# Graph attention and mixture of experts on one core: the second product three tiles behind the first, its results in three banks, ScalarE's output in four slots, rows turned sooner, and GpSimd's sends paced by the first products

## What is computed

```python
# x: 64 graphs x 128 nodes x 128 features; adj: 64 x 128 x 128
x = x + gnn(layernorm(x), adj, W, a)            # one graph attention layer
y = layernorm(x)
probs = softmax(y @ gate_w + gate_b)            # 16 experts
top_probs, top_idx = top_k(probs, 2)            # two experts for each node
gates = top_probs / sum(top_probs)
hidden = silu(y @ w1[e]) * (y @ w2[e])          # e: the expert, 128 -> 256
x = x + sum over both experts of gate * (hidden @ w3[e])
```

## Time and profile before

| | |
|---|---|
| median of three runs | 521.4 us (519.5 to 524.1) |
| the profiled execution | 522.0 us, span 520.2 us |
| PE / DVE / ACT / POOL busy | 395.9 / 250.4 / 226.7 / 257.1 us |
| attention part | to about 165 us |
| first pass of the experts | first product 168.3 us, last send 353.3 us |
| second pass | rows turned from 360.2 us, last send 513.7 us |
| granted clock of TensorE, mean | 0.913 |

### The profile page before, as it was taken

One profiled execution on the slowest core, in us unless ns is written; L12 is line 12 of the kernel. 1 busy time (PEld: TensorE's weight loads), 2 busy tenths in 40 slices (PEclk: granted clock), 3 DMA queues, 4 the chain that ended last, 5 costly groups with the idle time before them and its releaser, 6 DMA issues.

```text
span 520.2 us, 11474 instructions
## 1 busy us (share of the span) xinstructions
PE 395.9 (76%) x2993; PEld 358.6 (69%) x2994; DVE 250.4 (48%) x978; ACT 226.7 (44%) x583; POOL 257.1 (49%) x284
## 2 busy tenths in 40 slices
PE   6789788777786564488888798872988888788782
PEld 3578677665675464488788697762888878778781
DVE  4788989858676323324342343340342433333341
ACT  2789686656465212224342343330443443333430
POOL 5222256765357575334555545551355555455454
PEclk9999999978786776879999999995999899999996
DMA  3544445546462365686675666524654655555410
GB/s 109 150 135 126 119 134 173 162 152 205 116 197 97 112 216 190 218 258 212 216 223 165 200 198 201 173 70 111 207 176 148 190 173 182 163 156 187 151 33 2
DMA packets 75547, 83.35 MB, mean 160 GB/s; under 512 B 10564, under 2 KB 60111, under 8 KB 75504
## 3 DMA queue, kind: packets, MB, share of 16 engines
q1 hardware_dynamic: 66032, 61.58, 39.1%
q0 software_dynamic: 9472, 21.26, 11.6%
HBM read 36.06 MB, written 28.94 MB: 125 GB/s over the span
## 4 chain that ended last, share of the span: by engine, by line
PE 49%; DVE 14%; issue 14%; SPq 6%; ACT 5%; DMA 4%; another core or an unknown queue 3%; ACTq 2%; POOL 1%; POOLq 0%; DVEq 0%
PE bank L494 26%; PE bank L504 11%; PE bank L366 4%; SPq L298 3%; ACT em L626 2%; PE bank L414 2%; PE bank L416 2%; DVE stats L682 2%; DMA shared<-in_adj_dram 2%; DVE R L738 1%; PE bank L423 1%; DVE h L692 1%; DVE prob L929 1%; DVE R L935 1%
## 5 line engine op out<-in xcount | busy, mean ns | idle before, releaser
L494 PE MATMUL bank<-xT,w_t 128*128 128x128 f32 x1280 | 180.5, 287 | 14.7 <-DVE prob L929 7.6
L494 PEld LDWEIGHTS bank<-xT,w_t 128*128 128x128 f32 x1280 | 164.8, 201 | 18.6 <-DVE prob L929 9.7
L929 DVE TENSOR_TENSOR prob<-em,bank 128x256 f32<-128x256 f32 x160 | 67.3, 420 | 181.1 <-ACT em L626 110.9
L626 ACT ACTIVATE em<-bank 128x256 f32<-128x256 f32 x160 | 59.8, 382 | 184.5 <-PE bank L494 127.9
L504 PE MATMUL bank<-W,prob 128*128 x640 | 104.3, 287 | 40.4 <-DVE R L935 38.6
L504 PEld LDWEIGHTS bank<-W,prob 128*128 128x128 f32 x640 | 87.3, 198 | 48.8 <-issue 48.7
L1030 POOL DMA_INDIRECT out_dram<-R x80 | 78.3, 978 | 82.1 <-DVE R L935 62.6
L1030 POOL DMA_INDIRECT sorted_rows<-R x80 | 78.4, 980 | 79.8 <-DVE R L935 60.4
L1008 POOL DMA_INDIRECT sorted_rows<-R,ROW x64 | 62.7, 980 | 26.2 <-issue 17.6
L935 DVE SCALAR_TENSOR_TENSOR R<-bank,R 128x128 f32<-128x128 f32 x160 | 55.4, 346 | 33.4 <-PE bank L504 28.0
L999 POOL TENSOR_TENSOR rstd<-var_eps,half_neg 128x4 f32<-128x4 f32 x32 | 32.4, 1022 | 68.4 <-DVE var_eps L698 65.4
(11 more groups left out here) (129 smaller groups left out, 384.6 us busy)
## 6 DMA issues: line engine op xcount, KB each, us to landing
R<-sorted_rows SPq DMA_DIRECT2D x160, 130.0 KB
w_t<-W SPq DMA_DIRECT2D x80, 256.0 KB
W<-in_L_ffn_w_dram SPq DMA_DIRECT2D x48, 128.0 KB
sorted_rows<-pad SPq DMA_DIRECT2D x34, 130.0 KB
R<-in_x_dram SPq DMA_DIRECT2D x16, 256.0 KB
shared<-in_adj_dram SPq DMA_DIRECT2D x16, 256.0 KB
sorted_rows<-R POOLq DMA_INDIRECT x80
out_dram<-R POOLq DMA_INDIRECT x80
```

The costliest lines, as they stand in the source:

```text
L494: ins = nc.tensor.matmul(H[k][:, m * P:(m + 1) * P], w_t[:, par, k, m * P:(m + 1) * P], xT[:, par, k * P:(k + 1) * P], start=True, stop=True)
L626: nc.scalar.activation(sil[:, k % 2, :], H[k][:, 0:HC * P], ACT.Silu).then_inc(silu_ready, 1)
L929: V.tensor_tensor(hidT[:, k, :], sil[:, k % 2, :], H[k][:, HC * P:2 * HC * P], ALU.mult).then_inc(hid_ready, 1)
```

## The change

- `LAG, NO = 3, 3`: the second product and the adding stand three tiles behind the first instead of two, and the results rotate through banks 5, 6 and 7. `down` waits for `row_ready` of tile t - 3.
- `sil` has four slots (in `hT`) instead of two; `silu` waits for `hid_ready` of t - 4 instead of t - 2.
- `turn_rows` and `copy_rows` move from k = 1 to k = 0.
- Since bank 7 is now a result bank, tables 1 and 2 are turned into the bank that the first second product of quads 1 and 2 is about to use, and read from it just ahead of that tile's add.
- Five of the 25 last dispatches wait for first products: tiles 47, 51, 55, 59 and 63 for 1, 2, 5, 8 and 11 of them.

```diff
+    LAG, NO = 3, 3
-        sil = em[:].rearrange("p (k m) -> p k m", m=HC * P)
+        sil = hT[:].rearrange("p a (k m) -> p (a k) m", m=HC * P)
+        def out_bank(c, at, k):
+            return (at % RB * QT + k + c * NT) % NO
-            XP, H, O = bank[0], bank[1:5], bank[5:7]
+            XP, H, O = bank[0], bank[1:5], bank[5:5 + NO]
-            def down(c, q, k, e):
+            def down(c, q, at, k, e):
                 t = q * QT + (c * NT + k)
+                o = O[out_bank(c, at, k)]
                 pe.wait_ge(hid_ready, t + 1)
-                if c or later(q, 1) or k >= 2:
-                    pe.wait_ge(row_ready, t - 1)
+                if c or later(q, 1) or k >= NO:
+                    pe.wait_ge(row_ready, t - (NO - 1))
+                if c == 0 and isinstance(q, int) and q in (1, 2) and k == 0:
+                    turn_table(q, o)
...
-                        if k == 1 and not last:
+                        if k == 0 and not last:
                             turn_rows(c, q + 1, (at + 1) % RB, nth + (at + 1) // RB)
-                        if k >= 2:
-                            down(c, q, k - 2, e[k - 2])
+                        if k >= LAG:
+                            down(c, q, at, k - LAG, e[k - LAG])
                         elif not first:
-                            down(c, q - 1, k + 2, e_last[k])
+                            down(c, q - 1, at + RB - 1, k + (QT - LAG), e_last[k])
...
             def silu(t, k):
                 act.wait_ge(up_done, t + 1)
-                if later(t, 2):
-                    act.wait_ge(hid_ready, t - 1)
+                if later(t, QT):
+                    act.wait_ge(hid_ready, t - (QT - 1))
...
-                        if k == 1 and not last:
+                        if k == 0 and not last:
                             copy_rows(c, q + 1, 1 - par)
...
-                        if k >= 2:
-                            add_row(c, t + (k - 2), at % RB, k - 2)
+                        if k >= LAG:
+                            add_row(c, t + (k - LAG), at, k - LAG,
+                                    table=q if c == 0 and isinstance(q, int) and q in (1, 2) and k == LAG else None)
...
+            PACED = {8: 1, 12: 2, 16: 5, 20: 8, 24: 11}
             for m in range(t, NG):
+                if m - t in PACED:
+                    pool.wait_ge(up_done, PACED[m - t])
                 dispatch(m)
```

More of the change, by code:

```diff
@@ L623, in silu @@
                 act.wait_ge(up_done, t + 1)
[L624 to L626 removed]
+                if later(t, QT):
+                    act.wait_ge(hid_ready, t - (QT - 1))
+                nc.scalar.activation(sil[:, k, :], H[k][:, 0:HC * P], ACT.Silu).then_inc(silu_ready, 1)
             def copy_up(k, par, e):
@@ L857, in read_table @@
                 dve.wait_ge(cols_turned, l + 1)
-                V.tensor_copy(EID[0:1, first:first + ahead], RT[0:1, TABLE_AT[l][0]:TABLE_AT[l][0] + ahead])
-                V.tensor_copy(BLK[0:1, first:first + n], RT[0:1, TABLE_AT[l][1]:TABLE_AT[l][1] + n]).then_inc(table_ready, 1)
+                V.tensor_copy(EID[0:1, first:first + ahead], source[0:1, TABLE_AT[l][0]:TABLE_AT[l][0] + ahead])
+                V.tensor_copy(BLK[0:1, first:first + n], source[0:1, TABLE_AT[l][1]:TABLE_AT[l][1] + n]).then_inc(table_ready, 1)
             full, ceil = t_f[:, 0, :], t_f[:, 1:3, :].rearrange("p c e -> p (c e)")
@@ L903, in aside @@
                     columns(2, tile_no)
-                if q == 1 and k == 3:
-                    read_table(1)
-                if q == 3 and k == 0:
-                    read_table(2)
             first_stats(0, 0)
@@ L921, in _ @@
             count_rows()
-            H, O = bank[1:5], bank[5:7]
+            H, O = bank[1:5], bank[5:5 + NO]
             def gate_hidden(t, k):
@@ L928, in gate_hidden, with add_row @@
                     dve.wait_ge(down_done, t - (QT - 1))
-                V.tensor_tensor(hidT[:, k, :], sil[:, k % 2, :], H[k][:, HC * P:2 * HC * P], ALU.mult).then_inc(hid_ready, 1)
-            def add_row(c, t, slot, k):
+                V.tensor_tensor(hidT[:, k, :], sil[:, k, :], H[k][:, HC * P:2 * HC * P], ALU.mult).then_inc(hid_ready, 1)
+            def add_row(c, t, at, k, table=None):
                 dve.wait_ge(down_done, t + 1)
-                r = rows[:, slot * QT + k, :]
-                V.scalar_tensor_tensor(r[:, D:2 * D], O[k % 2][:, 0:D], r[:, GATE + c:GATE + c + 1], r[:, D:2 * D],
+                o = O[out_bank(c, at, k)]
+                if table is not None:
+                    read_table(table, o)
+                r = rows[:, at % RB * QT + k, :]
+                V.scalar_tensor_tensor(r[:, D:2 * D], o[:, 0:D], r[:, GATE + c:GATE + c + 1], r[:, D:2 * D],
                                        ALU.mult, ALU.add).then_inc(row_ready, 1)
@@ L949, in quad @@
                     if last:
-                        for k in (2, 3):
-                            add_row(c, t + k, at % RB, k)
+                        for k in range(QT - LAG, QT):
+                            add_row(c, t + k, at, k)
                 list_run(dve, quad, peel=(c == 0))
```

19 lines of the change are left out of this document (8 added, 11 removed).

## The result

The changed kernel takes 514.49 us, the median of six runs (509.41 to 519.98), the kernel before on the same chip 520.09 (six runs, 516.93 to 524.1). The ratio is 0.988, with a 95% interval of 0.984 to 0.993. Timed once more on another chip the ratio was 0.984 (0.979 to 0.989). So the change is faster by 1.2 to 1.6 %, where 3.3 % was forecast. The ratios leave out executions that fell into a slower state of the chip, so they are not always the quotient of the two medians beside them.

A forecast was written before the change was run, and what follows sets the result against it. The prediction took PE's signals, held back during bursts of GpSimd sends, to bound the kernel. From 522.0 us, -11 (steady), -9 (dispatches) and +2.6 (tails) gave 504.6, stated as 504.5; own range 490 to 515, with rivals 484 to 525.

The forecast's parts named there:

- What bounds the kernel: Both passes: bursts of GpSimd sends hold back PE's signals, so some 0.4 us of each tile are waiting, 140 tiles long.
- The steady term: Both passes, 140 tiles: a lag of three saves 0.08 us a tile, -11 us; bounds 0 and -56.
- cycles of five: Signals, burst, next signals: five sends for four, 8.93 us for five tiles where four took 7.65; one cycle in four keeps four.
- The transposes' place: Turning rows and their copy one place sooner in each quad takes back some saving: 0.04 us a tile.
- The paced dispatches: First pass's start: pauses in GpSimd's dispatches free SP's padding writes, so quad 4 loads sooner: -9 us, bounds -2 and -13.
- With both halves at 12.80 us, SP is through 8.0 us sooner: SP's 32 padding blocks before quad 4's load: the first 16 fall from 20.81 us to the others' 12.80.
- Tails: End of each pass: one send more behind the last product, 2 x 1.28 = +2.6 us.
- PE without waits: Rival: delayed signals come just in time and sends are single; 474 us, or 486 with six tiles a cycle; 15 in 100.
- Burst unchanged: Rival: the cycle keeps four tiles; 515.6 us, or 524.6 without the dispatches' gain; 15 in 100.
- The slower restart: Rival: copy and register load delay each cycle's restart; 9.9 us for five tiles, 525 to 535 us; 10 in 100.
- The first rival: PE runs nearly without waits: up to 1.55 us a tile for 474 us, 1.70 for 486; 15 in 100.
- The sum: Whole execution: 522.0 - 11 - 9 + 2.6 = 504.6 us, stated as 504.5.

The follow-up runs named there:

- few sends: Kernel before, with the sends of three tiles of four left out in the second pass: 494.56 us in one run against 528.74.
- thin sends: Kernel before, second pass's sends moving 16 bytes of each row instead of 512, to a scratch tensor: 525.48 us in one run against 528.74.
- The two pairs: Rows turned behind the quad's second tile again, on the changed kernel (0.977 for 0.984) and with padding dealt out and pauses kept (0.967 for 0.973).
- dealt-out padding: Changed kernel, SP's 16 second-pass padding writes moved from ahead of quad 4's load to two behind each of eight later loads: 0.973; without pauses 0.970.

## Why the prediction was right and wrong

**What bounds the kernel: right.** PE's signals wait for an end of GpSimd's sends. With few sends the lateness was gone (0.08 us) and PE ran at 1.45 us a tile; with thin sends it stayed. The third bank without the lag gave nothing (0.997). The Trainium skill's Perfetto Trace Analysis (Optimization Strategy) says that consistent bubbles can mean too little PSUM for the next tile; for PE's stops at second products this is not the cause here. Whether more banks would help the first products, ahead of which most stops stand with the lag, was not tried.

**The steady term: size near, its steps only in part.** Forecast -11; the two stretches of first products gave -9.2 and -4.7, together -13.9. Between tiles 84 and 156 a first product came every 1.853 us before and 1.770 after, 0.08 less as forecast. Between tiles 20 and 76, in the first pass, it was 1.899 and 1.742, twice the forecast 0.08; why more is saved there was not looked into, so that the term comes near is in part luck. The profiled execution has the cycles of five that were forecast: of the 14 whole cycles of the second pass that I cut out, 12 have five tiles, at 9.2 us where 8.93 was worked out; the late signals mostly came 0.8 to 1.4 us behind the burst, where 0.8 was taken. But in the profile of the second timing of the same kernel, 10 of 16 cycles have four tiles, 5 have five and one has six, and that kernel is as much faster (0.984). There a cycle of four takes 7.35 us, for 7.54 before, and a tile 1.800. On one chip, cycles of four take 7.24 us with the lag alone, 7.78 with the pauses alone and 7.83 with three banks and a lag of two. So the length of the burst is not what the saving hangs on; a shorter cycle does it as well. Why the cycle of four is shorter with the lag was not tested. The point where "each tile of lag is one send more" breaks was not in the prediction at all: four tiles gave 0.999.

**The transposes' place: not what I charged.** I took 0.04 us a tile for the transposes between the sends. The one price that the trace shows is at quad 4, where PE waits for rows one tile earlier. The two pairs point to some 3 us in all and don't settle it.

**The paced dispatches: the step that failed.** "With both halves at 12.80 us, SP is through 8.0 us sooner" took the second half as fixed, and with it the 10 us and the -9. The pauses did end the runs of dispatches, and the first half fell from 20.81 to 16.51 us, not to 12.80 (the pauses alone brought 12.39). But the tiles that PE finished sooner gave GpSimd nine sends in one run, from 200.66 on, just over SP's second half, which rose from 12.80 to 15.31 (10.80 with no sends over it). The load of quad 4 came 1.6 us sooner, the turn 2.5, and tile 14 not at all; of 9 us there remain 2.2, and those only if the start's scatter is taken off. In the second profile of the changed kernel the stretch to tile 14 is 56.7 us for 56.9. The text named this run of sends, and charged 1 us for it. Nor were the four writes in 1.93 us, which it calls undisturbed, a rate to count on: sixteen with GpSimd idle took 10.80. The deeper fault is that time won for SP was not time won for the kernel: with dealt-out padding the pauses again gave nothing (0.970 without, 0.973 with), and of the 12 us by which tile 14 came sooner with it about half reached the end (0.973 for 0.984). Pauses alone: 0.999.

**Tails: too small.** Forecast +2.6, measured +5.7. One send more behind each last product was priced at 1.28 us. But behind the first product of the last tile the kernel before has 5 sends left in either pass, and the changed one 7 in the first and 8 in the second. Every other kernel here with a lag of three has 7 or 8; those with a lag of two that send every tile have 5 or 6. These rows are the end of the changed kernel's second pass and of the first:

```profile
497.60 2.25 PE L512 MATMUL bank<-W,prob 128*128 x16
```
```profile
336.52 1.06 PE L499 MATMUL bank<-xT,w_t 128*128 128x128 f32 x8
337.41 1.06 PE L512 MATMUL bank<-W,prob 128*128 x8
341.59 2.05 PE L512 MATMUL bank<-W,prob 128*128 x8 [3.12 <-DVE R L940]
```

Of the four second products behind the last first product, all follow without a stop in the second pass; in the first pass the last two wait 3.12 us for an add, where in the kernel before they wait 1.79. Each pass pays 2.6 to 3.1 us in this profile, and up to 5.4 in the other kernels with a lag of three.

**The rivals.** PE without waits (474 to 486) did not come: GpSimd's sends still bunch, in fours and fives. "Burst unchanged" did not come as worked out either, for the lag gave its 1.6 % also where most bursts stayed at four. The slower restart did not come; cycles of five took 9.2 us, below the 9.55 from which it decides. The first rival's two times start from different rates, 1.85 us a tile for 474 and 1.91 for 486, so they are further apart than they look.

**The sum.** The steady term and the tails, -13.9 and +5.7, make -8.2 where -8.4 was forecast, by two errors that cancel. The sum of -17.4 was missed by the dispatches: 2.2 for 9, and 2.3 us of scatter at the start hide even these.

## What to carry to other kernels

Before a wait is costed as an engine's own work, look which engine's stream ends just ahead of it each time: here the late readers of PE started mostly 0.7 to 1.4 us behind GpSimd's last send, and leaving sends out was the quickest proof. Work that is freed on one engine runs over something else at once: when a queue (SP's here) is to be freed from an engine's bursts, list what that engine will issue in the new time, and charge it at the rate measured under such a burst. A block of transfers that nobody waits for yet can be dealt out in twos between those that someone waits for; here this was worth nearly as much again as the change itself (0.973 with the pauses and 0.970 without them, against 0.984).

## What the runs showed of the hardware

- While GpSimd issues indirect DMAs one behind the other (0.98 us each, 0.30 between), PE's semaphore signals reach ACT and DVE late, in the changed kernel's second pass by up to 5.2 us, and arrive together, mostly 0.7 to 1.4 us behind the last of them. 16 bytes a row instead of 512 change neither this nor the 0.98 us.
- SP's own DMA issues are slowed by the same runs: 16 writes of padding took 20.81, 21.60 and 21.64 us under dispatches without pause, 12.39 to 16.51 with pauses, 15.31 and 17.16 under nine sends in a row, 11.18 under five sends with gaps, and 10.80 with GpSimd idle.
- With GpSimd's sends thinned to one in four, PE's busy share in the trace went from 84 to 100 % and its granted clock from 0.98 to 1.00 of the upper level (2.4 GHz).
